# Edge attention of a graph layer: one stream of 768 edges with a window of 32 nodes, or two streams of 384 edges with windows of 16

## The chip, the cores and the metric

One core of one Trainium2 chip runs the whole kernel. The metric is the time of one execution on the device in microseconds.

## What is computed

A graph attention layer over 6250 nodes of 256 values and 200000 edges sorted by their target node, then a layer of 8 experts of which each node uses two. What matters here is the sum over edges:

```
K = enh @ Wk + bk ; V = enh @ Wv + bv ; Q = enh @ Wq + bq      # 4 heads of 64
scores = einsum('ehd,ehd->eh', Q[dst], K[src] + 0.2 * rel[kind]) / 8
ex = exp(scores - segment_max(scores, dst)[dst])
agg = segment_sum(ex / segment_sum(ex, dst)[dst] * V[src], dst)
```

## The kernel before

`prepare` normalises the nodes, computes Q (kept on chip, transposed, as QT), K and V (written to the table kv_dram) and lays out the edges: groups of G = 768 edges, NG = 261 of them. `edge_pass` walks over the groups. `nodes` divides the sums, adds the rest of the layer and picks the experts; `experts` runs them. If a group's edges don't fit its window, a slow pass in any order follows; the inputs don't call for it.

A group takes the edges in their order; its first edge's node is the base, and its scores are laid out as 128 rows (4 heads x W = 32 nodes from the base) by 768 columns (edges). Edges of other nodes are pushed down by a penalty of 2^100. At its end a group's sums [128 x 65] (64 values and the sum of weights, through a column of ones in the table's rows) and its maxima are carried into the next one, if that begins within the window, by a small matmul with a 0/1 matrix (carry).

Each engine runs the same loop over steps (`pipeline`, four steps to one turn of the loop, the rest written out), and semaphores are the only order between engines. Each step has work of several groups: a is the group to come, g the present one, c the one before, o the one five before on SP. The buffers are rings of R = 4.

- SP, per step: wait until the slot's gathers are over (s_kv), the list of 768 sources (L195); wait for VectorE's onehot of three groups back, the rows of kinds to 64 partitions (L200) and of places to 34 (L202); for group o a register load of the base (L206), a wait for the former group's writes, a wait for VectorE's sum (s_acc, by `hold`, L82), and four writes of 32 rows of 65 values to agg_dram (L213).
- POOL, per step: wait until psA of the group four before is over (s_agg), then for the list, then six gathers of 128 rows of 516 floats (L229).
- ScalarE: four copies of Q into qblock (L248, L252), half of the copies of K transposed (kT, L258), the carried sums scaled (L269), exp of the scores (L276) and of the maxima (L278), the transposed probabilities out of PSUM (L288).
- VectorE: the other half of kT (L308), carry (L318), onehot out of the rows (L323), the maximum of the scores (L329), maxima with the carried ones (L332, L335), the new sum (L341), the relation part of the query in two parts of float32r (L347, L349), the carried maximum (L351).
- PE: 12 transposes of K (psK, L369), the scores psD of two halves of 384 edges (two float32r matmuls, L387, and four of 64 rows, L392, each), the carried sums (L402) and 48 value matmuls of 32 rows by 65 columns (psA, L408: six tiles of edges x two times two heads, one head each), the carried maxima and the relation part (psX, L420, L423), six transposes of the probabilities (psP, L433). In a step the order is psK (first half), psD of g, psA of c, psK (second half), psX, psP of g.

Of the kernel before, what the change touches and what calls it, by code (L numbers as in the profile page):

```python
# [16 lines left out]
P = 128  # L17
# [5 lines left out]
W = P // H  # L23
TG = 6
G = TG * P
NG = -(-E // G)
GH = G // 2
CW = HD + 1
XW = D + 2
KVW = D + H * CW  # L30
# [4 lines left out]
QW = N + W + 22  # L35
# [49 lines left out]
def lay_constants():  # L85
# [5 lines left out]
    first = (((q % W) == 0)[None, :] & ((p // W)[:, None] == (q // W)[None, :])).astype(np.float32)  # L91
    pen = np.zeros((P, P), np.float32)
    for r in range(W + 2):
        pen[NREL + r] = np.where((q % W) == r, 0.0, -BIG)
    match = np.zeros((P, 1), np.float32)
    match[:NREL, 0] = np.arange(NREL)
    match[NREL:NREL + W + 1, 0] = np.arange(W + 1)
    match[NREL + W + 1, 0] = -1
    inwin = (p % W).astype(np.float32)[:, None]
    isfirst = ((p % W) == 0).astype(np.float32)[:, None]  # L100
    before = (p[:, None] < q[None, :]).astype(np.float32)
    parts = dict(ident=ident, first=first, pen=pen, before=before, ones=np.ones((P, P), np.float32),
                 match=match, inwin=inwin, isfirst=isfirst,
# [25 lines left out]
def edge_pass(nc, ctx, cst, QT, kv_dram, src_dram, featx_dram, feat_t_dram, agg_dram, bases, flag, penc, relT):  # L129
# [8 lines left out]
    R = 4  # L138
    NR = NREL + W + 2
    idx = [sb(f"e_idx{i}", [P, TG], I32) for i in range(R)]  # L140
    rows = [sb(f"e_rows{i}", [P, G], BF16) for i in range(R)]
    kv = [sb(f"e_kv{i}", [P, TG, KVW]) for i in range(R)]
    onehot = [sb(f"e_onehot{i}", [P, G], F32R) for i in range(R)]
    qblock = [sb(f"e_qblock{i}", [P, DC, P]) for i in range(R)]

    qrel = [[sb(f"e_qrel_{n}{i}", [P, P], F32R) for n in ("high", "low")] for i in range(R)]
    prob = [sb(f"e_prob{i}", [P, G]) for i in range(R)]
    probT = [sb(f"e_probT{i}", [P, TG, P]) for i in range(R)]
    carry = [sb(f"e_carry{i}", [P, P]) for i in range(R)]
    acc = [sb(f"e_acc{i}", [P, CW]) for i in range(R)]  # L150
    carried = [sb(f"e_carried{i}", [P, CW]) for i in range(R)]
    small = [sb(f"e_small{i}", [P, 8]) for i in range(R)]
# [3 lines left out]
    psP = ctx.enter_context(nc.psum_tensor("psP", [P, 2, 512], F32))  # L156
    psA = ctx.enter_context(nc.psum_tensor("psA", [P, 512], F32))
    psX = ctx.enter_context(nc.psum_tensor("psX", [P, 512], F32))
    MX, MC, MM, NM, AL = (slice(i, i + 1) for i in range(5))

    ident = cst("ident")
    s_idx = [sem(f"es_idx{i}") for i in range(R)]
    s_rows = [sem(f"es_rows{i}") for i in range(R)]
    s_kv = [sem(f"es_kv{i}") for i in range(R)]
    s_out = [sem(f"es_out{i}") for i in range(R)]
# [18 lines left out]
    LO, HI, WARM = -1, 2, 6  # L184

    with nc.Block() as blk:
        @blk.sync
        def _(sp):
            def step(T):
                g = T(0)  # L190
                if g.live:

                    if g.first >= R:
                        hold(sp, s_kv[g.slot], g.rnd * (16 * TG))
                    sp.dma_start(idx[g.slot][:, :], src_dram[bass.ds(g.t, 1)].rearrange("a (p t) -> (a p) t", t=TG)  # L195
                                 ).then_inc(s_idx[g.slot], 16)

                    if g.first >= R:
                        hold(sp, s_oh, g.t - (R - 1))
                    sp.dma_start(rows[g.slot][0:NREL, :],  # L200
                                 feat_t_dram[bass.ds(g.t, 1)].to_broadcast([NREL, G])).then_inc(s_rows[g.slot], 16)
                    sp.dma_start(rows[g.slot][NREL:NR, :],  # L202
                                 featx_dram[bass.ds(g.t, 1)].to_broadcast([W + 2, G])).then_inc(s_rows[g.slot], 16)
                o = T(5)
                if o.live:
                    base = sp.value_load(bases[0:1, bass.ds(o.t, 1)], min_val=0, max_val=N - 1)  # L206

                    if o.first >= 1:
                        b = T(6)
                        hold(sp, s_out[b.slot], (b.rnd + 1) * (16 * H))  # L210
                    hold(sp, s_acc, o.t + 1)
# [3 lines left out]
            pipeline(sp, NG, 0, 6, R, WARM, step)  # L215
            for i in range(R):
                sp.wait_ge(s_out[i], 16 * H * len(range(i, NG, R)))

        @blk.gpsimd
        def _(pool):  # L220
            def step(T):
                g = T(0)
                if g.live:

                    if g.first >= R:
                        pool.wait_ge(s_agg, g.t - (R - 1))
                    hold(pool, s_idx[g.slot], (g.rnd + 1) * 16)
# [5 lines left out]
            pipeline(pool, NG, 0, 0, R, WARM, step)  # L233

        @blk.scalar
        def _(act):
            act.preload_act_table(ACT.Exp)
            act.wait_ge(s_init, 3)

            def step(T):  # L240
                a = T(-1)
                if a.live:

                    base = act.value_load(bases[0:1, bass.ds(a.t, 1)], min_val=0, max_val=N - 1)
                    if a.first >= R:
                        hold(act, s_d, a.t - (R - 1))
                    for b in range(2):
                        act.copy(  # L248
                            qblock[a.slot][b * HD:(b + 1) * HD, :, :].rearrange(
                                "p a (h w) -> p a h w", w=W)[:, 0, b, :],  # L250
                            QT[b * HD:(b + 1) * HD, 0, bass.ds(base, W)])
                        act.copy(  # L252
                            qblock[a.slot][b * HD:(b + 1) * HD, :, :].rearrange(
                                "p a (h w) -> p a h w", w=W)[:, 1, 2 + b, :],
                            QT[b * HD:(b + 1) * HD, 1, bass.ds(base, W)]).then_inc(s_qb, 1)
# [10 lines left out]
                if c.live:  # L266
                    act.wait_ge(s_exp, c.t * 2 + 2)
                    act.wait_ge(s_agg, c.t + 1)
                    act.activation(carried[c.slot][:, :], psA[:, P:P + CW], ACT.Copy,  # L269
                                   scale=small[c.slot][:, AL]).then_inc(s_cas, 1)  # L270
                if g.live:
                    act.wait_ge(s_m, g.t * 3 + 3)

                    if g.first >= R:
                        act.wait_ge(s_pp, g.t * 2 - 2 * (R - 1))
                    act.activation(prob[g.slot][:, :].rearrange("p (c q) -> p c q", c=2), psD[:, :, 0:GH], ACT.Exp,  # L276
                                   bias=small[g.slot][:, NM], scale=SCALE).then_inc(s_exp, 1)
# [4 lines left out]
                if g.live:  # L282

                    if g.first >= R:
                        act.wait_ge(s_agg, g.t - (R - 1))
                    for j, (lo, hi) in enumerate(((0, 4), (4, TG))):
                        act.wait_ge(s_pp, g.t * 2 + j + 1)
                        act.copy(probT[g.slot][:, lo:hi, :].rearrange("p t q -> p (t q)"),  # L288
                                 psP[:, j, 0:(hi - lo) * P]).then_inc(s_pT, 1)
            pipeline(act, NG, LO, HI, R, WARM, step)  # L290

        @blk.vector
        def _(dve):
            for i in range(R):
                dve.memset(qblock[i][:, :, :], 0.0)
                dve.tensor_copy(qrel[i][0][:, :], cst("pen"))
# [1321 lines left out]
```

## Time and profile before

| | us |
|---|---|
| median of 3 runs | 4055.07 (4054.34 to 4059.47) |
| the profiled execution | 4048.79 |
| its span in the trace | 4046.9 |
| edge pass in it | about 197 to 2893 |
| prepare | 0 to 197 |
| nodes | 2893 to 3235 |
| experts | 3235 to 4047 |

From the page of the profile: PE is busy for 3305.5 us (82% of the span), VectorE (DVE) for 1565.8, ScalarE (ACT) for 1377.3, GpSimd (POOL) for 1952.5. The queue of gathers takes 41.9% of the 16 DMA engines' span, SP's queue 20.0%.

PE is TensorE's matmuls, PEld its weight loads, SPq a DMA issue on SP's queue. A row of a group gives the engine, the operation, output and input with their shapes, how many there were, busy us and mean ns of one, then the idle time ahead of them and what ended it. "remote" and "issue" are waits for which the profile shows no instruction's end. The ends of matmuls are modelled. POOL's busy time of a gather is the making of its descriptors, not the transfer.

### The profile page before, as it was taken

The page shows a single profiled execution, that of the slowest core. Times are in us where ns is not written, and L with a number is a line of the kernel's source. Part 1 is how long each engine was busy: PE and PEld are TensorE (multiplying, and loading weights), DVE is VectorE, ACT ScalarE, POOL GpSimd, SP SyncE. Part 2 cuts the span into 40 slices and gives each one's busy share as a digit, 9 for nine tenths or more (in the row PEclk, how much of TensorE's full clock was granted, in tenths as well). Part 3 has the DMA queues.
Part 4 walks back from the last instruction along what each step waited for, and adds up shares of the span by engine and source line. Part 5 has one row for each costly group of instructions (what it writes and reads, how often), then busy time and mean ns, then how long its engine had stood idle before and what let it go on. Part 6 is the DMA issues. An engine that isn't in the chain of part 4 may idle for free. (4 is left out here: it accounts for less than half of the span.)

```text
span 4046.9 us, 94323 instructions
## 1 busy us (share of the span) xinstructions
PE 3305.5 (82%) x27466; PEld 2408.9 (60%) x27466; DVE 1565.8 (39%) x4862; ACT 1377.3 (34%) x3933; POOL 1952.5 (48%) x2011
## 2 busy tenths in 40 slices
PE   6878787778788887787888788788676399999998
PEld 3545555555555555555555555555454288888887
DVE  7633333333333333333333333333498511111111
ACT  1223333333333333333333333333344322222222
POOL 3255555555555555555555555555356422222222
PEclk9979889889999889899899898999755599999999
DMA  7466666666666666666666666666455466666664
GB/s 236 156 169 173 173 172 173 172 174 174 173 172 174 171 174 173 173 174 174 173 173 172 172 174 173 174 174 173 129 159 151 148 201 185 187 187 185 187 182 112
DMA packets 416486, 698.44 MB, mean 173 GB/s; under 512 B 131663, under 2 KB 289127, under 8 KB 416278
## 3 DMA queue, kind: packets, MB, share of 16 engines
q0 software_dynamic: 148832, 452.92, 41.9%
q1 hardware_dynamic: 267590, 244.85, 20.0%
q14 instruction: 46, 0.38, 0.0%
q8 instruction: 18, 0.29, 0.0%
HBM read 625.14 MB, written 73.18 MB: 173 GB/s over the span
## 5 line engine op out<-in xcount | busy, mean ns | idle before, releaser
L229 POOL DMA_INDIRECT e_kv<-d_kv,e_idx x1566 | 1539.4, 983 | 1151.1 <-PE psA L408 735.0
L408 PE MATMUL psA<-e_kv,e_probT 128*32 128x65 f32 x12528 | 414.5, 237 | 478.7 <-issue 478.3
L408 PEld LDWEIGHTS psA<-e_kv,e_probT 128*32 128x32 f32 x12528 | 288.0, 117 | 575.8 <-issue 553.8
L308 DVE COPY e_kT<-psK 128x384 f32<-128x384 f32 x522 | 289.2, 554 | 738.9 <-remote 430.6
L258 ACT COPY e_kT<-psK 128x384 f32<-128x384 f32 x522 | 247.6, 474 | 929.6 <-remote 882.9
L369 PE MATMUL psK<-consts,e_kv 128*128 128x128 f32 x3132 | 516.7, 309 | 29.2 <-DMA e_kv<-d_kv,e_idx 25.8
L329 DVE TENSOR_REDUCE e_small<-psD 128x1 f32<-128x768 f32 x261 | 250.0, 958 | 722.2 <-remote 715.2
L1446 POOL DMA_INDIRECT out<-f_y,f_whose x112 | 174.1, 1554 | 646.9 <-DVE f_y L1499 625.3
L392 PE MATMUL psD<-e_kT,e_qblock 128*64 128x384 f32 x2088 | 454.1, 514 | 0.0
L369 PEld LDWEIGHTS psK<-consts,e_kv 128*128 128x128 f32 x3132 | 416.6, 162 | 61.8 <-issue 36.7
L1465 ACT ACTIVATE f_hT<-f_psH,f_b 128x256 f32<-128x256 f32 x448 | 212.5, 474 | 589.4 <-PE f_psH L1543 587.9
L1543 PE MATMUL f_psH<-f_xT,f_w 128*128 128x256 f32 x1792 | 397.7, 380 | 1.3 <-DVE f_xT L1485 1.3
L1533 PE MATMUL f_psY<-f_w,f_hT 128*128 128x256 f32 x1792 | 396.0, 379 | 0.0
L1543 PEld LDWEIGHTS f_psH<-f_xT,f_w 128*128 128x128 f32 x1792 | 341.6, 191 | 48.4 <-DMA f_w<-in_W 1.7
L1533 PEld LDWEIGHTS f_psY<-f_w,f_hT 128*128 128x128 f32 x1792 | 336.2, 190 | 43.4
L433 PE MATMUL psP<-consts,e_prob 128*128 128x128 f32 x1566 | 287.0, 332 | 31.1 <-issue 20.2
L288 ACT COPY e_probT<-psP 128x512 f32<-128x512 f32 (+1 forms) x522 | 229.8, 482 | 187.5 <-PE psP L433 130.2
L276 ACT ACTIVATE e_prob<-psD,e_small 128x768 f32<-128x768 f32 x261 | 235.2, 901 | 121.6 <-DVE e_small L335 113.2
L433 PEld LDWEIGHTS psP<-consts,e_prob 128*128 128x128 f32 x1566 | 210.7, 167 | 101.6 <-issue 69.4
L387 PE MATMUL psD<-e_onehot,e_qrel_high 98*128 98x384 f32 x522 | 227.3, 435 | 4.5 <-issue 4.5
L423 PE MATMUL psX<-e_qblock,relT 128*64 128x128 f32 x1044 | 209.5, 334 | 0.0
L269 ACT ACTIVATE e_carried<-psA,e_small 128x65 f32<-128x65 f32 x261 | 82.8, 317 | 361.3 <-PE psA L408 361.3
(201 smaller groups left out, 3679.4 us busy)
## 6 DMA issues: line engine op xcount, KB each, us to landing
f_w<-in_W SPq DMA_DIRECT2D x112, 1024.0 KB, 8.2
e_rows<-d_featt SPq DMA_DIRECT2D x261, 96.0 KB
e_kv<-d_kv,e_idx POOLq DMA_INDIRECT x1566
d_agg<-e_acc SPq DMA_DIRECT2D x1044, 8.1 KB
f_xs<-d_xs SPq DMA_DIRECT2D x56, 258.0 KB, 2.8
e_rows<-d_featx SPq DMA_DIRECT2D x261, 51.0 KB
d_kv<-p_kv SPq DMA_DIRECT2D x48, 258.0 KB, 2.7
d_agg<-p_zero POOLq DMA_DIRECT2D x10, 650.0 KB, 15.7
```

The lines of the kernel that those rows point to most:

```text
L229: pool.indirect_dma_start(out=kv[g.slot][:, t, :], out_offset=None, in_=kv_dram[:, :], in_offset=bass.IndirectOffsetOnAxis(ap=idx[g.slot][ ...
L258: act.copy(kT[a.slot % 2][:, 1, j * GH:(j + 1) * GH], psK[:, 1, 0:GH]).then_inc(s_kTa, 1)
L276: act.activation(prob[g.slot][:, :].rearrange("p (c q) -> p c q", c=2), psD[:, :, 0:GH], ACT.Exp, bias=small[g.slot][:, NM], scale=SCALE). ...
L288: act.copy(probT[g.slot][:, lo:hi, :].rearrange("p t q -> p (t q)"), psP[:, j, 0:(hi - lo) * P]).then_inc(s_pT, 1)
L308: dve.tensor_copy(kT[a.slot % 2][:, 0, j * GH:(j + 1) * GH], psK[:, 0, 0:GH]).then_inc(s_kTv, 1)
L329: dve.tensor_reduce(sm[:, MX], psD[:, :, 0:GH], AX.XY, ALU.max).then_inc(s_m, 1)
L369: mm = pe.transpose(psK[:, half, t * P:(t + 1) * P], kv[a.slot][:, third * 3 + t, half * P:(half + 1) * P], ident)
L392: mm = pe.matmul(psD[half, c, 0:GH], qblock[g.slot][:, b, half], kT[g.slot % 2][:, b, cols], start=False, stop=True, tile_position=(0, hal ...
L408: mm = pe.matmul(psA[h * W:(h + 1) * W, 0:CW], probT[c.slot][:, t, h * W:(h + 1) * W], kv[c.slot][:, t, D + h * CW:D + (h + 1) * CW], star ...
L433: mm = pe.transpose(psP[:, j, (t - lo) * P:(t - lo + 1) * P], prob[g.slot][:, t * P:(t + 1) * P], ident)
L1533: mm = pe.matmul(psY[:, t, 0:D], hT[:, f, t * P:(t + 1) * P], w2[c.slot][:, f, :], start=f == 0, stop=f == FC - 1)
L1543: mm = pe.matmul(psH[:, f % 4, 0:BT], w1[g.slot][:, a, f * P:(f + 1) * P], xT[g.slot][:, a, :], start=a == 0, stop=a == DC - 1)
```

## The change

Two streams of edges are worked on at once. Each is about half of the edges (they start at edge 0 and at edge 99776; 261 groups of 384 edges each), with its own base and a window of 16 nodes; the rows of the scores are 2 streams x 4 heads x 16 nodes = 128, the columns 384. A step still holds 768 edges, and there are still 261 steps.

- The rows of the table have 512 floats (K and V), without the columns of ones; the sum of weights comes from exp's accumulated output, [128 x 1].
- Values are multiplied two heads at a time: 24 matmuls of 32 rows (two heads of 16 nodes) by 128 columns. Of each result only one head's half is used; sums are [128 x 130].
- Scores of a step fill one bank of PSUM, two banks in turn: one float32r matmul for the windows (pen by inside, 36 rows), two for the relations (relhot, 128 rows: 64 kinds of each stream), eight for K on four column tiles of 32.
- kv, lists, carry, sums, carried and small have U = 6 buffers (4 before), the others R = 3 (4 before); the loop has six steps a turn.
- The lists of sources are laid out on chip by `prepare` (idxall: one copy and 13 transposes at its end), and ScalarE copies each step's [128 x 6] out of it, five steps ahead. The list's DMA per step and the source table in DRAM are gone.
- SP per step: rows to 2 x 64 and 2 x 18 partitions (four DMAs), two register loads, eight writes of 16 rows of 65.
- exp, reduce, onehot (now relhot and inside), the probability copy are 384 wide; VectorE's new sum is two operations, the relation part of the query four small ones.
- `prepare` computes places for both streams, with limits at the middle node; `nodes` reads V as 256 columns.

The core of the diff, cut:

```
-W = P // H
+W = 16
...
-KVW = D + H * CW
+ST = 2 * H
...
-    R = 4
...
+    U = 6
+    R = 3
...
-    LO, HI, WARM = -1, 2, 6
+    LO, HI, WARM = -1, 2, 8
+    AHEAD = U - 1
...
                     if g.first >= R:
-                        hold(sp, s_kv[g.slot], g.rnd * (16 * TG))
-                    sp.dma_start(idx[g.slot][:, :], src_dram[bass.ds(g.t, 1)].rearrange("a (p t) -> (a p) t", t=TG)
-                                 ).then_inc(s_idx[g.slot], 16)
-
-                    if g.first >= R:
-                        hold(sp, s_oh, g.t - (R - 1))
-                    sp.dma_start(rows[g.slot][0:NREL, :],
-                                 feat_t_dram[bass.ds(g.t, 1)].to_broadcast([NREL, G])).then_inc(s_rows[g.slot], 16)
-                    sp.dma_start(rows[g.slot][NREL:NR, :],
-                                 featx_dram[bass.ds(g.t, 1)].to_broadcast([W + 2, G])).then_inc(s_rows[g.slot], 16)
+                        hold(sp, s_oh, (g.t - (R - 1)) * 2)
+                    for c in range(2):
+                        sp.dma_start(kinds[g.slot % R][c * NREL:(c + 1) * NREL, :],
+                                     feat_t_dram[bass.ds(g.t, 1), c, :].to_broadcast([NREL, GH])
+                                     ).then_inc(s_rows[g.slot], 16)
+                        sp.dma_start(places[g.slot % R][c * (W + 2):(c + 1) * (W + 2), :],
+                                     featx_dram[bass.ds(g.t, 1), c, :].to_broadcast([W + 2, GH])
+                                     ).then_inc(s_rows[g.slot], 16)
...
-                    for h in range(H):
-                        sp.dma_start(agg_dram[bass.ds(base, W), h, :], acc[o.slot][h * W:(h + 1) * W, :]
-                                     ).then_inc(s_out[o.slot], 16)
...
+                    hold(sp, s_acc, o.t * 2 + 2)
+                    for c in range(2):
+                        for h in range(H):
+                            p0, odd = c * HW + h * W, h % 2
+                            sp.dma_start(agg_dram[bass.ds(base[c], W), h, :],
+                                         acc[o.slot][p0:p0 + W, odd * CW:(odd + 1) * CW]).then_inc(s_out[o.slot], 16)
...
-                    if g.first >= R:
-                        pool.wait_ge(s_agg, g.t - (R - 1))
-                    hold(pool, s_idx[g.slot], (g.rnd + 1) * 16)
+                    if g.first >= U:
+                        pool.wait_ge(s_agg, g.t - (U - 1))
+                    hold(pool, s_idx, g.t + 1)
...
+                n = T(-AHEAD)
+                if n.live:
+
+                    if n.first >= U:
+                        act.wait_ge(s_kv[n.slot], n.rnd * (16 * TG))
+                    act.copy(idx[n.slot][:, :].rearrange("p (c j) -> p c j", c=2),
+                             idxall[:, 0:2 * NG * TS].rearrange("p (c q) -> p c q", c=2)[:, :, bass.ds(n.t * TS, TS)]
+                             ).then_inc(s_idx, 1)
...
+                    pe.matmul(scores, pen[:, :], inside[g.slot % R][:, :], start=True, stop=False)
+                    for part in qrel[g.slot % R]:
+                        pe.matmul(scores, part[:, :], relhot[g.slot % R][:, :], start=False, stop=False)
...
-                    for j, (lo, hi) in enumerate(((0, 4), (4, TG))):
-                        pe.wait_ge(s_pT, c.t * 2 + j + 1)
-                        for t in range(lo, hi):
-                            for h in range(H):
-                                mm = pe.matmul(psA[h * W:(h + 1) * W, 0:CW], probT[c.slot][:, t, h * W:(h + 1) * W],
-                                               kv[c.slot][:, t, D + h * CW:D + (h + 1) * CW],
-                                               start=t == 0, stop=t == TG - 1, tile_position=(0, h * W))
...
+                    pe.wait_ge(s_pT, c.t + 1)
+                    for j in range(TS):
+                        for s in range(2):
+                            for b in range(DC):
+                                own = slice((s * DC + b) * 32, (s * DC + b + 1) * 32)
+                                mm = pe.matmul(psA[own, 0:2 * HD], probT[c.slot % R][:, j, own],
+                                               kv[c.slot][:, s * TS + j, D + b * P:D + (b + 1) * P],
+                                               start=j == 0, stop=j == TS - 1, tile_position=(0, own.start))
```

## Rows read from the trace of the kernel before

**Rows 1.** Busy time by stretch: length, then PE, PEld, DVE, ACT, POOL, clock, DMA.
```profile
230.00:2915.00 2685.00, 2151.68 (x22417) 1460.94 (x22418) 1013.43 (x2877) 991.09 (x2863) 1521.20 (x1551) 0.90 0.63 171
```

**Rows 2.** Groups and what ended their waits, 400 to 3000 us.
```profile
L229 POOL DMA_INDIRECT e_kv<-d_kv,e_idx x1450 | 1426.1, 984 | 1046.5 <-PE psA L408 678.1 <-issue 368.3
...
L408 PE MATMUL psA<-e_kv,e_probT 128*32 128x65 f32 x11760 | 388.3, 238 | 451.2 <-issue 450.9 <-ACT e_probT L288 0.3
...
L329 DVE TENSOR_REDUCE e_small<-psD 128x1 f32<-128x768 f32 x244 | 233.7, 958 | 669.6 <-remote 665.3 <-PE psD L392 4.3
```

**Rows 3.** Timeline of POOL, one step: start us, length us, idle before.
```profile
2025.95 0.95 POOL L229 DMA_INDIRECT e_kv<-d_kv,e_idx  x1 [3.02 <-PE psA L408]
...
2030.99 1.33 POOL L229 DMA_INDIRECT e_kv<-d_kv,e_idx  x1 [0.30 <-issue]
2032.63 0.96 POOL L229 DMA_INDIRECT e_kv<-d_kv,e_idx  x1 [0.30 <-issue]
2036.12 0.95 POOL L229 DMA_INDIRECT e_kv<-d_kv,e_idx  x1 [2.54 <-PE psA L408]
```

**Rows 4.** Timeline of PE, one step at full clock.
```profile
2022.35 0.43 PE L402 MATMUL psA<-e_acc,e_carry 128*128 128x65 f32 x2
2022.72 0.43 PE L408 MATMUL psA<-e_kv,e_probT 128*32 128x65 f32 x15
2024.33 0.76 PE L408 MATMUL psA<-e_kv,e_probT 128*32 128x65 f32 x33 [1.18 <-issue]
...
2028.31 0.43 PE L387 MATMUL psD<-e_onehot,e_qrel_high 98*128 98x384 f32 x1
...
2028.84 0.87 PE L392 MATMUL psD<-e_kT,e_qblock 128*64 128x384 f32 x4
...
2030.98 0.44 PE L402 MATMUL psA<-e_acc,e_carry 128*128 128x65 f32 x2
```

**Rows 5.** Timeline of VectorE, the same steps.
```profile
2024.52 0.96 DVE L329 TENSOR_REDUCE e_small<-psD 128x1 f32<-128x768 f32 x1 [1.89 <-remote]
...
2030.88 0.61 DVE L323 TENSOR_SCALAR e_onehot<-e_rows,consts 98x768 fp32r<-98x768 bf16 x1
2034.75 0.96 DVE L329 TENSOR_REDUCE e_small<-psD 128x1 f32<-128x768 f32 x1 [3.25 <-remote]
```

**Rows 6.** Timelines of PE, VectorE and POOL in the fill, and PE after it.
```profile
213.73 0.65 PE L423 MATMUL psX<-e_qblock,relT 128*64 128x128 f32 x4
...
224.31 0.28 DVE L347 CAST e_qrel_high<-psX 64x128 fp32r<-64x128 f32 x1 [10.77 <-remote]
...
228.95 0.96 POOL L229 DMA_INDIRECT e_kv<-d_kv,e_idx  x1 [0.30 <-issue]
...
242.88 0.89 PE L408 MATMUL psA<-e_kv,e_probT 128*32 128x65 f32 x48
```

**Rows 7.** Timeline of SP's DMA issues in the fill and behind it.
```profile
218.94 0.34 SPq L195 DMA_DIRECT2D e_idx<-d_src  x1
232.66 0.48 SPq L200 DMA_DIRECT2D e_rows<-d_featt  x1
233.19 0.43 SPq L202 DMA_DIRECT2D e_rows<-d_featx  x1
244.70 1.90 SPq L213 DMA_DIRECT2D d_agg<-e_acc  x4
```

**Rows 8.** SP's loads of line 206, 400 to 2800 us: ns min/median/max.
```profile
L206 SPq TENSOR_LOAD <-bases x234: 3/440/710, 406.3 to 2793.1; - x117
```

**Rows 9.** Timeline of SP's DMA issues in the steady state.
```profile
2036.64 2.27 SPq L213 DMA_DIRECT2D d_agg<-e_acc  x4
2040.35 0.69 SPq L195 DMA_DIRECT2D e_idx<-d_src  x1
...
2043.34 0.00 SPq L202 DMA_DIRECT2D e_rows<-d_featx  x1
```

**Rows 10.** What SP waited for, 400 to 2800 us: us, times, longest.
```profile
SPq L82 <- DVE e_acc L341: 88.3, 71, 1.8
```

**Rows 11.** A group of VectorE in prepare, 0 to 60 us.
```profile
L655 DVE TENSOR_REDUCE p_misfit<-p_place 128x1 f32<-128x768 f32 x2 | 1.9, 953 | 0.1
```

More of the change, by code:

```diff
@@ L34 @@
 LAST = N - P
-QW = N + W + 22
+QW = N
 AR = 50 * P
@@ L136, in sem @@
         return ctx.enter_context(nc.semaphore(name))
-    R = 4
[L139 to L144, printed above, removed]
-    qrel = [[sb(f"e_qrel_{n}{i}", [P, P], F32R) for n in ("high", "low")] for i in range(R)]
[L147 to L152, printed above, removed]
+    U = 6
+    R = 3
+    idx = [sb(f"e_idx{i}", [P, TG], I32) for i in range(U)]
+    kinds = [sb(f"e_kinds{i}", [P, GH], BF16) for i in range(R)]
+    places = [sb(f"e_places{i}", [MR, GH], BF16) for i in range(R)]
+    kv = [sb(f"e_kv{i}", [P, TG, 2 * D]) for i in range(U)]
+    relhot = [sb(f"e_relhot{i}", [P, GH], F32R) for i in range(R)]
+    inside = [sb(f"e_inside{i}", [MR, GH], F32R) for i in range(R)]
+    qb = [sb(f"e_qb{i}", [P, P]) for i in range(R)]
+    qrel = [[sb(f"e_qrel_{n}{i}", [P, P], F32R) for n in ("high", "low")] for i in range(R)]
+    pen = sb("e_pen", [MR, P], F32R)
+    prob = [sb(f"e_prob{i}", [P, GH]) for i in range(R)]
+    probT = [sb(f"e_probT{i}", [P, TS, P]) for i in range(R)]
+    carry = [sb(f"e_carry{i}", [P, P]) for i in range(U)]
+    acc = [sb(f"e_acc{i}", [P, 2 * CW]) for i in range(U)]
+    carried = [sb(f"e_carried{i}", [P, 2 * CW]) for i in range(U)]
+    small = [sb(f"e_small{i}", [P, 8]) for i in range(U)]
     kT = [sb(f"e_kT{i}", [P, DC, G]) for i in range(2)]
@@ L155, in edge_pass @@
     psD = ctx.enter_context(nc.psum_tensor("psD", [P, 2, 512], F32))
-    psP = ctx.enter_context(nc.psum_tensor("psP", [P, 2, 512], F32))
+    psP = ctx.enter_context(nc.psum_tensor("psP", [P, 512], F32))
     psA = ctx.enter_context(nc.psum_tensor("psA", [P, 512], F32))
     psX = ctx.enter_context(nc.psum_tensor("psX", [P, 512], F32))
-    MX, MC, MM, NM, AL = (slice(i, i + 1) for i in range(5))
+    MX, MC, MM, NM, AL, SUM = (slice(i, i + 1) for i in range(6))
+    CARRIED = slice(256, 256 + 2 * CW)
     ident = cst("ident")
[L162 to L165, printed above, removed]
+    pairs = lambda a: a.rearrange("p (o c) -> p o c", o=2)
+    s_idx = sem("es_idx")
+    s_rows = [sem(f"es_rows{i}") for i in range(U)]
+    s_kv = [sem(f"es_kv{i}") for i in range(U)]
+    s_out = [sem(f"es_out{i}") for i in range(U)]
     s_init = sem("es_init")
@@ L219, in _ @@
+            pipeline(sp, NG, 0, 6, U, WARM, step)
+            for i in range(U):
+                sp.wait_ge(s_out[i], 16 * ST * len(range(i, NG, U)))
         @blk.gpsimd
@@ L285, in step @@
                         act.wait_ge(s_agg, g.t - (R - 1))
-                    for j, (lo, hi) in enumerate(((0, 4), (4, TG))):
[L287 to L290, printed above, removed]
+                    act.wait_ge(s_pp, g.t + 1)
+                    act.copy(probT[g.slot % R][:, :, :].rearrange("p t q -> p (t q)"), psP[:, 0:GH]).then_inc(s_pT, 1)
+            pipeline(act, NG, -AHEAD, HI, U, WARM, step)
         @blk.vector
@@ L367, in k_turned @@
                         pe.wait_ge(s_kTa if half else s_kTv, a.t * 2 + third)
-                    for t in range(3):
+                    for t in range(TS):
                         mm = pe.transpose(psK[:, half, t * P:(t + 1) * P],
-                                          kv[a.slot][:, third * 3 + t, half * P:(half + 1) * P], ident)
+                                          kv[a.slot][:, third * TS + t, half * P:(half + 1) * P], ident)
                     mm.then_inc(s_pk, 1)
```

422 lines of the change are left out of this document (240 added, 182 removed).

## The prediction, made before the changed kernel had run

> **What bounds the kernel now.** I read the busy times by stage first. The edge pass holds 2685 of 4047 us, in it PE's matmuls are busy for 2152 us, POOL for 1521 and VectorE and ScalarE for about 1000 each, at a mean granted clock of 0.90 [rows 1]. So PE looks like the bound. The table of waits says otherwise. POOL waits 678 us for psA's matmuls, but those matmuls themselves stand still for 451 us with no releaser ("issue"), and VectorE's reduce of the scores waits 665 us for something called "remote", work that PE's records show as over [rows 2]. POOL's 1450 gathers there, six a step, are 241.7 steps in 1426.1 busy and 1046.5 idle us: a period of 10.23 us, times 261 steps the 2670 us of the pass.
>
> One period, in order. psA of a step ends, POOL wakes and issues six gathers at a pitch of 1.26 us (0.96 busy, 0.30 issue, one of 1.33), 2025.95 to 2033.6, and the next six begin at 2036.12, 10.17 us after the first [rows 3]. The scores' matmuls of the same step start at 2028.31 and are over by about 2031.0, where PE goes on to L402 [rows 4]; VectorE sees them only at 2034.75, 1.2 us after the last gather [rows 3, 5]. Then psA ends and the next gathers start. PE's 48 value matmuls show the same: 15 go out in 0.43 us, then 1.18 us of nothing, until VectorE's reduce (2024.52) shows the scores as arrived [rows 4, 5]; where no gather is under way all 48 take 0.89 us without a gap [rows 6]. In the fill of the ring, 24 gathers without a pause up to 229.9, PE's psX matmuls start at 213.73 and VectorE reads the result at 224.31, 10 us later [rows 6]. I call this the freeze: while gathers are being issued and their data still drain, PE's completions come late. It doesn't follow PE's clock: the period stays near 10.2 us while PE's nominal step is 8.6 us at full clock.
>
> SP is caught in it too. Its issues for a step are four writes of the sums (L213), the list of sources (L195), two broadcasts of rows (L200, L202) and one load (L206). With no gather under way they cost: three pitches of L213 in 1.90 us, 0.63 each (0.48 if the entry holds four), L200 and L202 0.53 and 0.45, L195 0.34 (that one in the fill), the load 0.44 (a median over the pass) [rows 7, 8]. With 0.35 us for the waits and registers between, that is 4 x 0.55 + 0.53 + 0.45 + 0.34 + 0.44 + 0.35 = 4.3 us of work. In the steady state it fills 2036.64 to 2043.34 and, with L202 and the load behind it, about 2044.6: 8.0 us [rows 9]. Its wait for VectorE's sum (L341) is 88.3 us in 234 steps, 0.38 us a step, in 71 of them [rows 10]. So SP has little left: 8.0 us occupied at least, and 10.23 - 0.38 = 9.85 at most, if nothing that the trace hides lies between.
>
> **The change, part by part.** Steps stay 261, gathers six a step, each row 2048 instead of 2064 bytes: POOL's floor is 6 x 1.26 = 7.56 us (7.9 with one or two long ones) as before. Nothing is won there.
>
> PE: value matmuls 48 to 24 at twice the columns, one bank of scores with three wide matmuls for four, eight kT matmuls on four column tiles for eight on two, transposes of the probabilities 6 to 3. From the rows, at full clock: values 0.89 at most [rows 6], the wide ones 3 x 0.27 (two of them from 2028.31 to 2028.84), kT 0.87 to twice that, the rest some 3 us: what is left of 8.6 without stall, values, wide ones and kT. The nominal step (2022.35 to 2030.98 now) falls from 8.6 to between 5.5 and 6.5 us [rows 4]. PE isn't what ends last, so this alone is worth nothing: the step waits for the freeze's end. VectorE's reduce halves from 0.96 us [rows 5] and ScalarE's exp too: both lie behind the freeze's end and ahead of psP, not ahead of the next gathers in a ring that is full, so at most 1 us a step, which I leave to the rivals.
>
> SP, which the change makes longer: eight L213 for four (each half the rows; the rows show no lower price for a smaller one: L202 with 34 partitions costs nearly what L200 with 64 does [rows 7]), four broadcasts for two, two loads for one, and no L195. At free speed +4 x 0.55 + 2 x 0.5 - 0.34 + 0.44 + 0.2 (register work of the second load) = +3.5 us a step (3.2 to 3.8 with L213 at 0.48 to 0.63), together 7.8 us. Occupied time so goes from 8.0 to 11.5 at the lower end and from 9.85 to 13.4 at the upper, as long as the six gathers of a step take the same time from it. I take 12.4, nearer to neither: the wait is nil in most steps, which speaks for the upper end, but a gather that starts later than now finds more of SP's work done at free speed, which speaks for the lower. Queued behind SP's writes are the next broadcasts; for those VectorE waits (relhot and inside), for VectorE's products PE, for psA POOL. The deeper ring (six) can't help: a ring evens out waits, and this is a rate. The removed wait of SP for s_kv (moved to ScalarE's list copy, five steps ahead) frees nothing on a queue that is full.
>
> ScalarE and VectorE: ScalarE gets an idle-time copy of 128x6 and loses half its exp and a copy; VectorE has three more small operations. Both are busy about 1000 of 2685 us [rows 1], so their cost is nil; if the cover were gone it would be under 0.5 us a step.
>
> Outside the loop: the first fill has 36 gathers for 24, 12 x 1.26 = +15 us [rows 3], less what of it SP's slower pace would hide, 0 to 15. Prepare: twice as many edge operations on VectorE, each half as wide (0.95 us at 768 [rows 11]), seven small ones, four more DMAs for edges and sources and the turning of the lists at its end, against four memsets and two operations gone: by the same row some ten such operations either way, -3 to +8 us; I take +3. The node stage reads rows of 256 for 260: nothing.
>
> A rule of the Trainium skill speaks the other way on SP's queue: the page "DMA: Bandwidth & Descriptors", section "Issuing engines are not separate DMA queues", says that the time a sequencer takes to initiate a DMA is usually small relative to the DMA itself. By it the five added DMAs a step would cost next to nothing, and the time would be that of the second rival below; the trace disagrees, with seven DMAs and a load filling 8 of 10.2 us [rows 9]. A second rule: the Trainium skill's page "SBUF — State Buffer", section "Who interferes with whom", says that VectorE in its two-port mode shuts GpSimd out of descriptor making. The trace agrees: the gather of 2030.99 takes 1.33 us for 0.96 beside L323 of 2030.88 [rows 3, 5]. The change has two such operations of half the width; one more hit a step would be 0.37 us, 97 us in all if POOL were the bound, nothing where SP is.
>
> **The sum.** (12.4 - 10.23) x 261 = +566; +15 for the fill; +3 for prepare: 4048.8 + 584 = 4633 us on the profiled execution, which stands 6.3 us under the median of the runs shown, so 4639 against 4055. With 11.5 and 13.4 us and the other bounds the case itself runs from 4380 to 4900.
>
> **The rivals.**
> *SP's queue (the forecast, slower), 0.50.* Decides as soon as SP's occupied time passes 10.23 us. For it: the 71 waits of 234, the unchanged gathers. Against: nobody waited for SP in the trace of before, so what slows it is seen only in its own stretches.
>
> *The freeze shrinks (faster), 0.38.* If PE's late completions and SP's slow pace come from the number of instructions and small packets that compete with the gathers, then a third fewer matmul pairs (86 to 56), full 2048-byte rows and no L195 lift a part of it. Then POOL's 7.6 to 7.9 us or SP's free 7.8 us is the floor; with some freeze left I take 8.6: (8.6 - 10.23) x 261 = -425, 4055 + 18 - 425 = 3648 us; 8.0 gives 3491, 9.4 gives 3856. For it: PE's free step of 5.5 to 6.5 and six buffers, which let POOL run on while a step's completions are late. Against: in the fill nothing but gathers runs and the freeze is at its deepest (10 us) [rows 6].
>
> *The gather cycle stays (no change), 0.10.* SP keeps up, but the ring is always full, so that every period is psA's end, 0.8, six gathers 7.65, 1.1 of drain, 0.6 of psA: 10.15 us. Then 4055 + 18 - 21 = about 4050, within 4035 to 4090, on either side of today's time.
>
> *The change isn't what runs*, 0.02: the nodes of a group don't fit a window of 16 and the slow pass in any order is taken, far above 4900. From the inputs, 384 edges reach over 13 nodes in the mean and 15 at most, so that I hardly believe it.
>
> **Chances.** A difference under 0.2% (8 us) can hardly be told from no change. Faster: 0.38 and a third of the third case, 0.41. Within 0.2%: 0.03. Slower: 0.50 + 0.04 + 0.02 = 0.56. The range has to take in both signs: from 3570 (under it about 0.08, the lower part of the second case) to 4860 (over it about 0.08). The likeliest case's own is 4380 to 4900.
>
> **What would show each step.** Right: a period near 12.4 us in POOL's gathers; POOL and PE waiting, at the end of the chain, for rows (VectorE relhot on a DMA of e_kinds or e_places); SP's wait for the sums gone; reduce and exp at half their time; the values' 24 matmuls within 0.9 us. Wrong: a period under 9.9 us; an L213 pitch under 0.7 us in the steady state; "remote" and "issue" waits that fall far below the 665 and 451 us [rows 2]. If the period is 10.1 to 10.3 with SP waiting, the third case holds. The forecast fails most easily at the assumption that gathers take the same time from SP as before.

## The result, and the profile after

The changed kernel took 4618.33 us (median of 4, 4614.54 to 4622.68) against 4055.43: a ratio of 1.139, 95% interval 1.137 to 1.141. The forecast was 4639.

From the page of the changed kernel, its groups (engine, operation, shapes, count, busy us, mean ns, idle time ahead and what ended it):

```profile
span 4620.7 us, 85700 instructions
...
PE 3469.6 (75%) x19652; PEld 2434.0 (53%) x19652; DVE 1654.1 (36%) x5938; ACT 1305.9 (28%) x4194; POOL 1920.7 (42%) x2017
...
L239 POOL DMA_INDIRECT e_kv<-d_kv,e_idx x1566 | 1503.2, 960 | 1693.5 <-PE psA L436 1276.6
L340 DVE TENSOR_SCALAR e_relhot<-e_kinds,consts 128x384 fp32r<-128x384 bf16 x261 | 115.9, 444 | 1833.7 <-DMA e_places<-d_featx 1833.7
```

The largest wait is a new one: VectorE waits 1833.7 us, 7.0 us a step, for the last of SP's broadcasts. The same by line from 400 to 3400 us, to be set beside [rows 2]:

```profile
L239 POOL DMA_INDIRECT e_kv<-d_kv,e_idx x1460 | 1401.4, 960 | 1596.3 <-PE psA L436 1225.3 <-issue 371.0
...
L436 PE MATMUL psA<-e_kv,e_probT 128*32 128x128 f32 x5832 | 341.9, 390 | 24.4 <-issue 24.4
```

1460 gathers are 243.3 steps in 2997.7 us: 12.32 us a step. The stall of 451 us in the value matmuls is 24 us now, and VectorE's reduce has no "remote" wait left (ScalarE's copies of kT keep 176.3 us of it). The bursts of gathers say 12.25 us for the whole pass (the first after the fill at 292.18, the last at 3403.05, 254 steps).

SP's DMA issues, in the steady state, to be set beside [rows 9], and VectorE's and POOL's lines of the same step:

```profile
2008.69 7.87 SPq L223 DMA_DIRECT2D d_agg<-e_acc  x8
2016.84 0.51 SPq L206 DMA_DIRECT2D e_kinds<-d_featt  x1
2017.45 0.48 SPq L209 DMA_DIRECT2D e_places<-d_featx  x1
2018.11 0.49 SPq L206 DMA_DIRECT2D e_kinds<-d_featt  x1
2018.69 0.45 SPq L209 DMA_DIRECT2D e_places<-d_featx  x1
2021.07 7.49 SPq L223 DMA_DIRECT2D d_agg<-e_acc  x8
...
2021.00 0.42 DVE L340 TENSOR_SCALAR e_relhot<-e_kinds,consts 128x384 fp32r<-128x384 bf16 x1 [7.39 <-DMA e_places<-d_featx]
...
2014.25 0.95 POOL L239 DMA_INDIRECT e_kv<-d_kv,e_idx  x1 [0.30 <-issue]
2019.50 0.95 POOL L239 DMA_INDIRECT e_kv<-d_kv,e_idx  x1 [4.30 <-PE psA L436]
```

As far as the trace shows, SP never stops: eight writes (7.87 us), 0.28, four broadcasts (2.30), loads and waits (1.93), 12.38 us in this step. The table of its waits between 400 and 3400 us is empty, where [rows 10] had 88.3 us. VectorE's relhot starts 2.3 us after the last broadcast was issued; behind it stand the maxima, psX and the rest of PE's step, and POOL waits for those. (This is one step; over the steps from 400 to 2800 us the eight writes take 7.7 us in the mean.)

Where the 574 us between the two spans went:

| stretch | before | after | difference |
|---|---|---|---|
| start to the first gather | 199.6 | 231.2 | +31.5 |
| first gather to the last psA | 2693.8 | 3220.3 | +526.5 |
| nodes and experts | 1153.5 | 1169.2 | +15.7 |

### The profile page after: what moved, and what is told of

Read it like the earlier page. It is cut to its first block and busy times, and to the rows that moved or that the text cites. A ratio compares the mean times of both kernels' runs of the same rounds, so it can differ in the third digit from the quotient of the medians.

```text
span 4620.7 us, 85700 instructions
## 1 busy us (share of the span) xinstructions
PE 3469.6 (75%) x19652; PEld 2434.0 (53%) x19652; DVE 1654.1 (36%) x5938; ACT 1305.9 (28%) x4194; POOL 1920.7 (42%) x2017
## 5 line engine op out<-in xcount | busy, mean ns | idle before, releaser
L340 DVE TENSOR_SCALAR e_relhot<-e_kinds,consts 128x384 fp32r<-128x384 bf16 x261 | 115.9, 444 | 1833.7 <-DMA e_places<-d_featx 1833.7
L448 PE MATMUL psX<-e_small,e_carry 128*128 128x1 f32 x522 | 129.4, 317 | 814.7 <-DVE e_small L354 411.3
L394 PE MATMUL psK<-consts,e_kv 128*128 128x128 f32 x3132 | 668.9, 373 | 34.4 <-issue 17.7
L394 PEld LDWEIGHTS psK<-consts,e_kv 128*128 128x128 f32 x3132 | 544.5, 199 | 123.0 <-issue 122.6
L448 PEld LDWEIGHTS psX<-e_small,e_carry 128*128 128x128 f32 x522 | 110.5, 264 | 881.1 <-issue 869.9
L293 ACT ACTIVATE e_prob<-psD,e_small 128x384 f32<-128x384 f32 x261 | 151.4, 580 | 968.9 <-DVE e_small L354 511.4
L436 PE MATMUL psA<-e_kv,e_probT 128*32 128x128 f32 x6264 | 370.9, 387 | 42.3 <-issue 41.8
L418 PE MATMUL psD<-e_kT,e_qb 128*32 128x384 f32 x2088 | 374.1, 808 | 0.0
L267 ACT COPY e_qb<-QT 64x32 f32 x1044 | 226.2, 217 | 321.6 <-issue 303.1
L429 PEld LDWEIGHTS psA<-e_acc,e_carry 128*128 128x128 f32 x522 | 125.0, 298 | 303.2 <-issue 303.2
## 6 DMA issues: line engine op xcount, KB each, us to landing
d_agg<-p_zero POOLq DMA_DIRECT2D x10, 650.0 KB, 14.9
```

The lines of the kernel that those rows point to most:

```text
L267: act.copy(qb[a.slot % R][o * HD:(o + 1) * HD, :].rearrange("p (c b o w) -> p c b o w", c=2, b=DC, o=2)[:, c, :, o, :], QT[o * HD:(o + 1) ...
L394: mm = pe.transpose(psK[:, half, t * P:(t + 1) * P], kv[a.slot][:, third * TS + t, half * P:(half + 1) * P], ident)
L418: mm = pe.matmul(psD[own, g.slot % 2, 0:GH], qb[g.slot % R][:, own], kT[g.slot % 2][:, b, c * GH:(c + 1) * GH], start=False, stop=True, ti ...
L436: mm = pe.matmul(psA[own, 0:2 * HD], probT[c.slot % R][:, j, own], kv[c.slot][:, s * TS + j, D + b * P:D + (b + 1) * P], start=j == 0, sto ...
L448: pe.matmul(psX[:, 0:1], carry[a.slot][:, :], small[(a.slot - 1) % U][:, MM], start=True, stop=True)
```

## The experiments

Each set ran on one chip, beside the kernel before, and no two sets on the same one. The first and the third set saw 4048.8 and 4048.6 us for it, the second 3637 us (3617 to 3682): that difference is a finding of its own, below. The kernels that leave gathers out or narrow them (n_none, n_narrow, n_half, r_none, r_narrow) were run once each, and their sums aren't the layer's. Steps are worked out as above, from POOL's busy and idle time over its gathers.

### First set: the number of issues on SP

**a_rows2**, the four broadcasts in two:

```
-                    for c in range(2):
-                        sp.dma_start(kinds[g.slot % R][c * NREL:(c + 1) * NREL, :],
-                                     feat_t_dram[bass.ds(g.t, 1), c, :].to_broadcast([NREL, GH])
...
+                    sp.dma_start(kinds[g.slot % R][:, :],
+                                 feat_t_dram[bass.ds(g.t, 1), :, :].rearrange("a c e -> (a c) e").unsqueeze(1
+                                 ).to_broadcast([2, NREL, GH])).then_inc(s_rows[g.slot], 16)
```

> The changed kernel with the four broadcasts of a step put into two DMAs (kinds of both streams in one, places in the other); same bytes, same partitions, same waits. Theory S (SP's queue is full, the time is the number of its instructions): two issues at about 0.6 us each fall away, 1.2 us of 12.3 a step, 261 steps: 4618 - 313 = about 4305 us, between 4280 and 4400. Theory L (VectorE waits for the landing of rows, which the DMA engines make late because of the packets and bytes): packets and bytes are the same, so 4600 to 4640.

Measured: 4404.56 us, 1.087 of before (1.086 to 1.089): 356 us over its before, where the change had cost 563, so 207 us less. A step of 11.46 us, 0.9 less. Theory L falls for the changed kernel: bytes and partitions are the same here, and the time went down with the issues. SP's queue has 424 packets a step for 470, but the changed kernel's rows don't land late: its relhot starts 1.7 us (mean, 400 to 2300 us) after SP is done with the last broadcast, and without gathers (r_none, below) it is 1.5. Theory S had the sign right, but the gain is a third smaller than its 313 us, and the time lies just above its range. Two things take from it. SP's broadcasts now meet gathers and cost more: in two steps of this trace (2000.01 and 2010.37 us) the second comes 2.4 and 1.7 us after the first instead of 0.6. And the merged rows do land late, 4.1 us after SP is done with them.

**a_writes2**, the eight writes in two. Before they leave, VectorE picks each row's own half of psA:

```
-                    for c in range(2):
-                        for h in range(H):
-                            p0, odd = c * HW + h * W, h % 2
-                            sp.dma_start(agg_dram[bass.ds(base[c], W), h, :],
-                                         acc[o.slot][p0:p0 + W, odd * CW:(odd + 1) * CW]).then_inc(s_out[o.slot], 16)
+                    for c in range(2):
+                        sp.dma_start(agg_dram[bass.ds(base[c], W), :, :].rearrange("w h q -> h w q"),
+                                     acc[o.slot][c * HW:(c + 1) * HW, :]).then_inc(s_out[o.slot], 16)
...
+                    dve.scalar_tensor_tensor(out=held[c.slot][:, :], in0=psA[:, 0:HD], scalar=cst("even"),
+                                             in1=carried[c.slot][:, 0:HD], op0=ALU.mult, op1=ALU.add
...
+                    dve.scalar_tensor_tensor(out=acc[c.slot][:, 0:HD], in0=psA[:, HD:2 * HD], scalar=cst("odd"),
+                                             in1=held[c.slot][:, :], op0=ALU.mult, op1=ALU.add).then_inc(s_acc, 1)
```

> The changed kernel with the eight writes of sums put into two, one for a stream: VectorE picks each row's half of the sums with two 0/1 columns, so that a sum is [128 x 65] again, and 64 rows of 65 go out in one DMA. One VectorE operation more, the same bytes written. Theory S: six issues of about 0.98 us fall away, so that SP needs 12.3 - 5.9 = 6.4 us, and another bound shows: between 8.0 (gathers back to back) and 10.2 us a step (gather cycle), 3490 to 4080 us. Theory L (packets): 4580 to 4640, since the packets of 260 bytes are as many as before.

Measured: 4114.31 us, 1.0165 (1.0145 to 1.0185). Six issues fewer take back 497 of the 563 us that the change had cost. (The edit also narrows the carried sums and their matmul from 130 to 65 columns, and SP's queue has 350 packets a step for 470; the expectation had put them as equal.) A step is 10.32 us. SP isn't relieved yet: its table of waits from 400 to 2800 us is still empty, and VectorE still waits longer for rows than for scores:

```profile
L348 DVE TENSOR_REDUCE e_small<-psD 128x1 f32<-128x384 f32 x233 | 128.2, 550 | 265.0 <-remote 262.1 <-PE psD L421 2.7
L340 DVE TENSOR_SCALAR e_relhot<-e_kinds,consts 128x384 fp32r<-128x384 bf16 x232 | 100.1, 431 | 951.0 <-DMA e_places<-d_featx 812.8 <-issue 125.6 <-DMA e_kinds<-d_featt 8.1
```

So the 6.4 us that theory S left to SP were too few. The issues that remain fall beside gathers and fill the step as far as the trace shows, and two bounds lie close together here: SP's rows and the late completions.

**a_both**, both merges.

> Both merges together: SP has four DMAs and two loads a step. Theory S: SP is no longer a bound, so the time is that of a_writes2 or at most 2% below it; if a_writes2 was still bound by SP (its rows late), then up to 1.2 us a step less, 300 us. Theory L: 4580 to 4640.

Measured: 4161.00 us, 1.028 (1.026 to 1.030), in the third set again (r_both) 4168.42, 1.030. A step of 10.54 us. Only here is SP relieved: VectorE's relhot waits for no rows any more, SP's waits come back (78.4 us on VectorE's sum, 51.4 on its inside), and so does the picture of [rows 2] and [rows 5], in the trace of a_both from 400 to 2800 us and around one step:

```profile
L438 PE MATMUL psA<-e_kv,e_probT 128*32 128x128 f32 x5472 | 427.7, 315 | 561.4 <-issue 560.4
...
2003.50 0.84 PE L438 MATMUL psA<-e_kv,e_probT 128*32 128x128 f32 x19
2006.48 0.27 PE L438 MATMUL psA<-e_kv,e_probT 128*32 128x128 f32 x1 [2.13 <-issue]
2008.93 0.69 PE L438 MATMUL psA<-e_kv,e_probT 128*32 128x128 f32 x4 [2.19 <-issue]
...
2009.11 0.56 DVE L347 TENSOR_REDUCE e_small<-psD 128x1 f32<-128x384 f32 x1 [6.08 <-remote]
```

PE has 56 pairs of weight load and matmul a step for 86, its scores were written by 2003.2 by its own records, and VectorE still sees them at 2009.11. So the change, freed of its own new bound, doesn't make the kernel faster: it comes back to a cycle like that of before, 10.54 us for 10.23. Why a_both is 1.1% slower than a_writes2, with two issues fewer, no trace explains; that stays open.

**b_write1**, the kernel before with its four writes in one:

```
-                    for h in range(H):
-                        sp.dma_start(agg_dram[bass.ds(base, W), h, :], acc[o.slot][h * W:(h + 1) * W, :]
-                                     ).then_inc(s_out[o.slot], 16)
+                    sp.dma_start(agg_dram[bass.ds(base, W), :, :].rearrange("w h q -> h w q"), acc[o.slot][:, :]
+                                 ).then_inc(s_out[o.slot], 16)
```

> The kernel before with the four writes of sums in one DMA, nothing else. Theory G (before is bound by the cycle of gathers and late completions, SP has just room enough): three issues of 0.6 to 1 us fall away on a queue with 0.38 us of wait a step, SP then waits 2 to 3 us a step more, and the time stays within 1% of 4055. Rival (SP was the bound of before too): -2 to -2.5 us a step or more, 3400 to 3550 us. A third possibility: fewer instructions on SP in the stretch of gathers shorten the late completions of PE by themselves: 3800 to 4000.

Measured: 4067.85 us, 1.0046 (1.0029 to 1.0063). SP's waits, 400 to 2800 us:

```profile
SPq L82 <- DVE e_acc L340: 592.6, 224, 6.7
```

Theory G holds. Three issues fewer became waiting time, 2.6 us in each of 224 waits, where [rows 10] had 0.38 us a step. In the kernel before SP was no bound; it was next to one.

### Second set: what the gathers take from others

**n_none**, the changed kernel without gathers (diff: the six DMAs give way to a copy of the list), and again as **r_none** in the third set.

> The changed kernel without its gathers (rows of the table are a constant set once; POOL only copies the step's list, so the sums are not the layer's). All of SP's 12 DMAs and two loads a step stay. Prediction's term to be measured: SP's free pace. Theory S with the freeze from the gathers: L223 at 0.48 to 0.63 us each, a step of 7.8 us (7.2 to 8.4), 4618 - 4.5 x 261 = about 3440 us (3290 to 3600). Rival (the 0.98 us of a write is its own price whatever the gathers do): 12.3 us a step stays, 4600.

Measured: 3615.09 us, and r_none 3615.95, just above the range of theory S (3290 to 3600) and far under the rival's 4600. SP in the trace of r_none, and VectorE's wait for its rows from 400 to 2400 us:

```profile
1501.53 3.87 SPq L224 DMA_DIRECT2D d_agg<-e_acc  x8
1505.74 0.51 SPq L207 DMA_DIRECT2D e_kinds<-d_featt  x1
1506.35 0.48 SPq L210 DMA_DIRECT2D e_places<-d_featx  x1
1507.01 0.48 SPq L207 DMA_DIRECT2D e_kinds<-d_featt  x1
1507.59 0.45 SPq L210 DMA_DIRECT2D e_places<-d_featx  x1
1509.89 3.87 SPq L224 DMA_DIRECT2D d_agg<-e_acc  x8
...
1518.77 3.86 SPq L224 DMA_DIRECT2D d_agg<-e_acc  x8
...
L339 DVE TENSOR_SCALAR e_relhot<-e_kinds,consts 128x384 fp32r<-128x384 bf16 x235 | 98.7, 420 | 943.0 <-DMA e_places<-d_featx 943.0
```

This is the disputed price alone. SP is the bound here too: its table of waits is empty, and VectorE waits for rows in every step. SP's free step is 8.6 us in these rows (1501.53 to 1518.77 are two) and 8.5 in the mean of the trace. Against the changed kernel only one term differs by much: eight writes in 3.87 us instead of 7.5 to 7.9 (7.33 in one of r_after); the broadcasts take 2.3 us in both, loads and waits 1.9. The gathers' price on SP is 12.25 - 8.5 = 3.8 us a step, nearly all of it in the writes, which are what runs beside the gathers.

**n_narrow**, a_both with rows of 256 bytes, as many as before:

```
-                            out=kv[g.slot][:, t, :], out_offset=None, in_=kv_dram[:, :],
+                            out=kv[g.slot][:, t, 0:64], out_offset=None,
+                            in_=kv_dram.rearrange("n (a b) -> (n a) b", b=64),
```

> a_both (four DMAs and two loads on SP a step) with gathers of the same number of rows, each 256 bytes instead of 2048 (the rest of the tile is a constant, so the sums are not the layer's). Theory D (the late completions come from the data on the DMA engines, 61% of their time here): POOL's pace stays 1.26 us a gather, the cycle loses its drain and its freeze: 7.7 to 8.5 us a step, 3450 to 3660 us. Theory P (they come from POOL's making and ringing of descriptors, whose number is the same): 10 to 10.5 us a step, 4050 to 4170.

Measured: 3404.95 us, 7.59 us a step, POOL back to back, even under theory D's range. Theory D seemed to hold. But it ran where the kernel before took 3637 us, and had no a_both beside it; the third set settles it, the other way.

**n_half**, a_both with three gathers of six.

> a_both with three gathers a step instead of six, full rows (half of the tile is a constant, so the sums are not the layer's). Both theories D and P: the stretch of gathers is 3.8 us instead of 7.6. If completions stand still during gathers and come in the rest (the cycle of the prediction), a step is at 10.4 - 3.8 = 6.6 us, 3170 us, unless PE's own 7 to 8 us at the low clock end it: 3250 to 3500. If the number of gathers isn't what sets the cycle: above 3900.

Measured: 2887.26 us, 5.64 us a step. That is under all the numbers expected: on this chip three gathers hold up nothing, and PE's step is shorter than I had put it here. PE is busy for 1252.7 of the 1300 us from 400 to 1700, at a granted clock of 1.00, so 5.64 us is PE's own step, within the 5.5 to 6.5 of the prediction. The run says nothing of the freeze.

**a_ahead3**, the changed kernel with POOL three groups behind psA instead of six:

```
-                    if g.first >= U:
-                        pool.wait_ge(s_agg, g.t - (U - 1))
+                    if g.first >= 3:
+                        pool.wait_ge(s_agg, g.t - 2)
```

> The changed kernel in which POOL waits for the step three back instead of six, so that only half of the deeper ring is used. Prediction: a ring evens out waits and doesn't change a rate, and SP's rate is the bound: within 0.5% of 4618. If the depth gave something: 4700 to 5000.

Measured: 5949.41 us, far outside what I expected. PE, POOL and SP in its trace:

```profile
1515.65 1.54 PE L394 MATMUL psK<-consts,e_kv 128*128 128x128 f32 x6 [8.60 <-DMA e_kv<-d_kv,e_idx]
...
1505.63 0.95 POOL L239 DMA_INDIRECT e_kv<-d_kv,e_idx  x1 [10.42 <-PE psA L436]
...
1511.92 0.95 POOL L239 DMA_INDIRECT e_kv<-d_kv,e_idx  x1 [0.30 <-issue]
...
1505.92 3.87 SPq L223 DMA_DIRECT2D d_agg<-e_acc  x8
```

The groups a, g and c are in use at once, so three slots leave no gather ahead: PE waits 8.6 us for the rows, POOL then 10.4 us for PE, 17.5 us a step. Before had one group ahead with its ring of four. My sentence that a ring evens out waits and isn't a rate holds only above the number in use. The last line is worth more: SP's eight writes take 3.87 us here in the midst of six gathers, the price of n_none. On this chip the gathers take nothing from SP's writes.

### Third set: the same again on one chip

> The changed kernel itself once more, beside the three others of this set on one chip. The kernel before took 3617 to 3682 us on the chip of the last set, against 4048 to 4055 on the two before it, so a chip has its own size of the late completions. Theory S: SP's 12 DMAs and two loads fill the step whatever the chip, never under the 8.6 us that they take without any gather (3615 us); where before takes 4050, this takes 4618; where before takes 3630, the freeze takes less from SP and this lies between 3700 and 4400, slower than before on either chip.

> a_both again (four DMAs and two loads on SP). If the chip is one where before takes 4050: 4160, as in the first set. If before takes 3630: SP is no bound and the gather cycle is short, POOL's 7.6 to 8.3 us: 3400 to 3650.

> The changed kernel without its gathers (rows a constant, so the sums are not the layer's), again. Theory S: SP's free pace doesn't depend on the chip: 8.6 us a step, 3600 to 3640 us.

> a_both with gathers of 256 bytes a row instead of 2048 (the rest of the tile is a constant, so the sums are not the layer's), beside r_both on the same chip. Theory D (late completions come from the gathers' data): POOL back to back, 3390 to 3450 us, and clearly below r_both where before takes 4050. Theory P (from the descriptors, as many as before): within 2% of r_both.

Measured, with the kernel before at 4048.55 us: r_after 4572.55 (1.129, 1.127 to 1.131), 1% under the first measurement of the changed kernel; r_both 4168.42 and r_none 3615.95, as expected; r_narrow 4158.34. Two results:

SP's free pace is the same on both chips (3615.09 and 3615.95), its pace beside gathers isn't: eight writes 7.33 us in r_after, 3.87 in a_ahead3. Those are two kernels, but one and the same shows it too: from the issue of the kinds to that of the places SP takes 1.6 to 1.7 us in r_narrow (around 1510 us) and 0.75 in n_narrow.

r_narrow is within 0.3% of r_both, at a quarter of the DMA engines' time. The queues and groups of r_narrow, 400 to 2400 us:

```profile
q0 software_dynamic: 36771, 37.73, 14.1%
...
L443 PE MATMUL psA<-e_kv,e_probT 128*32 128x128 f32 x4608 | 351.8, 314 | 440.5 <-issue 439.3
...
L352 DVE TENSOR_REDUCE e_small<-psD 128x1 f32<-128x384 f32 x192 | 107.0, 557 | 1015.6 <-remote 1015.6
```

and the same of r_both, and of n_narrow (400 to 3000 us or to the end), the same program as r_narrow on the other chip:

```profile
q0 software_dynamic: 91068, 298.48, 61.5%
...
L347 DVE TENSOR_REDUCE e_small<-psD 128x1 f32<-128x384 f32 x190 | 106.0, 558 | 1008.9 <-remote 1008.9
```

```profile
L352 DVE TENSOR_REDUCE e_small<-psD 128x1 f32<-128x384 f32 x244 | 136.0, 557 | 246.2 <-PE psD L425 246.2
```

Theory P holds against D: with 61.5% or 14.1% of the engines' time in gathers VectorE waits the same 5.3 us a step for a completion that PE's records show as over. With the same program on the other chip that wait is 1.0 us, and its releaser is a plain PE instruction. The queue's packets fell too, from 91068 to 36771. So the late completions go with what stayed the same, the number of gathers and of the rows they fetch, and not with bytes or packets; which of those two, no run separates. They showed on the chips of the first and the third set and not on that of the second, which was seen in one set only, so that its state at the time can't be told from the chip itself. What makes them, no run shows.

No version that computes the layer beats the kernel before where that takes 4050 us. Whether a_both would on the chip where it takes 3637 was not tried; n_narrow's 3404.95 only says that little but the gathers' data could stand in the way.

## Why the prediction was right, and where not

**The bound before** (gathers and late completions, SP with little left): right, by b_write1 and by the return of the same picture in a_both.

**SP becomes the bound**: right. The queue has no wait, VectorE waits for the broadcasts, and the time follows the issues (a_rows2, a_writes2).

**The size, 12.4 us a step**: measured 12.25 to 12.32, by two terms that were off and cancelled, which is luck. SP's free work was put at 7.8 us and is 8.5 (r_none): two loads with the waits around them take 1.9 us for my 1.43, and four broadcasts 2.3 for 1.98, while eight writes with the gap behind them take 4.2 for 4.4 (the entry of 1.90 us held four at 0.48, and I had taken 0.55). What the gathers add was put at 3.7 to 5.5 us, 4.6 in the value taken, and is 3.8, near the lower bound. A likely reason is that in the changed kernel the broadcasts fall into the 4 to 6 us in which POOL waits, and cost their free price; the upper bound had counted everything that SP's table doesn't list as occupied time.

**The total**, 4639 for 4618, is closer than its terms, again by luck: the pass grew by 526.5 us and not by 581, prepare by 31.5 and not by 3, nodes and experts by 15.7 and not by nothing. And the case that came true had been given 0.50.

**Fill, +15**: right. From the first gather to the first burst behind the fill it is 45.0 us before and 61.0 after, 16.0 more. What I had left out is the other end: behind the last burst SP's queue runs without gathers, and those steps are shorter: the last four psA before take 28.2 us for 40.9 at the steady pace, the last six after 48.4 for 73.5, which gives 12.3 us back. The two nearly cancel, so that 261 times the change of the step (2.01 us by the bursts) gives 525 of the 526.5 us.

**Prepare, +3 (-3 to +8)**: +31.5, the step that failed. I counted VectorE's operations and not where the chain now waits. In the trace of the changed kernel, and the first node tile in that of before:

```profile
37.06 0.17 DVE L688 CAST p_mid<-p_mid_i 128x2 f32<-128x2 int32 x1 [32.12 <-DMA p_mid_i<-in_dst]
...
67.67 0.43 DVE L748 BATCH_NORM_STATS2 p_stat<-p_x 128x6 f32<-128x256 f32 x1
...
35.22 0.43 DVE L686 BATCH_NORM_STATS2 p_stat<-p_x 128x6 f32<-128x256 f32 x1
```

The middle node is needed first, and its DMA is the last of the 17 for whose semaphore the chain waits at its head, until 37.06; before, VectorE worked through the edges from 11.15 on, and needed the 14 DMAs of then only behind them. It stands 32 us, and the first node tile begins 32.4 us later than before. The edge operations, the part that I had counted, grew from 14.9 us (11.15 to 26.05) to 17.8 (38.47 to 56.29), by just the 3 us forecast.

**Nodes, 0**: +15.7 for nodes and experts together, not looked into.

**The rivals**: "the freeze shrinks" can't be told from the time of the changed kernel alone, but a_both shows that it didn't shrink with fewer matmuls, no list DMA and rows of 2048 bytes; the step is 10.5 us. "The gather cycle stays" (10.15 us, 4050) comes near it. (a_writes2, at 10.3 us, says less, since SP still held its step.) One of the signs that I had named as speaking against the forecast was a wrong sign: the "issue" and "remote" waits did fall (451 to 24 us), probably because in a step of 12.3 us the late completions fall into time in which PE waits for SP's rows anyway. And one sign of being right failed without harm: the 24 value matmuls take 1.51 us (in the step of 2017.11) and not 0.9, as PE's terms were for full clock.

**The rules of the skill**: that the time to initiate a DMA is usually small relative to the DMA (the Trainium skill, "DMA: Bandwidth & Descriptors", "Issuing engines are not separate DMA queues") would have given no loss from more issues; here six issues fewer of the same bytes are worth some 500 us, and the measurement decides. The lockout of GpSimd by VectorE's two-port mode ("SBUF — State Buffer", "Who interferes with whom", the Trainium skill) cost nothing to speak of: the mean gather is 960 ns in the changed kernel.

## What to carry to other kernels

Count a queue's issues as an engine's work: sum its free pace from a stretch without gathers, compare it with the period, and ask before adding DMAs whether several with the same source pattern can be one. The price of an issue isn't a constant: it doubled beside the gathers, and after six issues were taken away those left still filled the step. A stretch in which a queue seems occupied but has little work has to be split by an experiment that removes the suspected cause; here leaving out the gathers gave the free term, and the difference the other one. And a wait that is moved to the head of a chain costs what the whole chain had covered.

## What the runs showed of the hardware

The same program on one core differed by 10% and more between sets that ran on different chips: the kernel before took 4048 to 4055 us in three and 3617 to 3682 in one, the narrow-gather program 4158 and 3405. Without gathers the two chips agree (3615.95 and 3615.09), so it isn't the pace of the engines by themselves. Where the kernel before takes 4050 us, VectorE waits for scores that PE's records show as written (2.7 us a step in the kernel before, 5.3 in r_both), and SP's writes beside gathers take twice their time (0.96 us in the mean for 0.48). The wait of VectorE doesn't depend on the bytes gathered (5.3 us in r_narrow too). A comparison of two kernels is only good on one chip.

The granted clock in the changed kernel's edge pass was 0.65 against 0.90 before [rows 1], with PE busy for 2313 us of 3205 instead of 2152 of 2685. Six psK transposes take 1.49 to 1.54 us at 1.2 GHz (2011.97 and 2018.55 us in the changed kernel) and 0.82 to 0.88 at 2.4 (2025.02 and 2027.73 us in the kernel before). SP's queue set the step here and doesn't wait for PE, so that this wasn't on the path.
